# Value sums of the cross attention, head by head in four 32-column groups of TensorE

## The chip, the core and the metric

The kernel runs on one core of a Trainium2 chip. The engines are PE (TensorE: matmuls, with its weight loads shown apart as PEld), DVE (VectorE), ACT (ScalarE), POOL (GpSimd) and SP (SyncE, which only issues DMAs here). They run side by side and wait for each other through semaphores. The metric is the device time of one execution in microseconds (us).

## The reference, cut to what matters

A perceiver block on x [32, 32, 512] with a context of 257 rows per batch item: cross attention, then a causal linear attention, then a mixture of experts. Only the first part is touched:

```python
qm, km, vm = (_split_heads(...) for q, k, v)        # 16 heads of 32
scores = einsum('bnlh,bnph->bnlp', qm, km) / sqrt(32)
attn = softmax(scores, axis=-1)                     # over 257 context rows
out = einsum('bnlp,bnph->bnlh', attn, vm)           # <- the value sums
out = out.transpose(0, 2, 1, 3).reshape(B, L, 512)
return out @ Wo.T + bo
```

For each batch item and head, the value sums are a product of a [32 queries, 257] matrix of probabilities with [257, 32] values. Everything is fp32.

## The kernel before, in words

There are two stages. Stage A (to about 830 us) does both attentions, the router and part of the shared expert; stage B does the experts. Only stage A is touched.

Stage A walks over 32 batch items, as passes t of four items b, and each item has six steps k. Each engine has the same steps written out in order (`per_batch(t, b, k, ...)`), and behind a step stand pieces of later work (`on_post`, `on_pre`) at fixed places: the table POST says for instance that "oproj", the output projection of the four items of the pass before, comes at step 6, which is b=1, k=0. So the order on each engine is written by hand and does not adapt; the engines meet at semaphores alone.

For item n, steps 0 to 3 project the keys (lines 856 to 858: three matmuls of 256 moving columns with split weights), steps 4 and 5 the values (872 to 874). Softmax and value sums of an item are carried into the steps of the next. For the item before, DVE scales the probabilities (L599), PE transposes them (L840) in two halves j of 128 context rows, and ACT copies them out as `att[:, j, :]` (L473). `att` is [128 context rows, 2, 512], where the 512 columns are 16 heads x 32 queries. The values stand in `vb[pb]` as [128 context rows, 2, 512], where 512 is 16 heads x 32.

At k=5 PE forms the value sums. It takes four heads at a time, g = 0 to 3: 128 columns of values as weights and 128 columns of probabilities as the moving operand, first half j=0 (L888), then j=1 (L889) added to it. The product is 128 x 128: each of the four heads' values against each of the four heads' probabilities. Only the four 32 x 32 blocks on the diagonal are wanted. The last context row (257th) is held apart as a vector `vlc`, since the values are taken relative to that row. Right behind, PE computes two score matmuls of the current item (L901), for which DVE waits (L644).

DVE then reads the diagonal blocks in `attended`: four adds (L613), each on 32 partitions and 4 x 32 elements, of the block and `vlc`, into `ot`, the operand of oproj (L946). PE waits for `s_od` (`av_copied`) before oproj and before the value sums of the next item overwrite the accumulator `av_ps`. One wait of PE for DVE's adds stands also in the shared expert's L1013, which uses the same bank at the end of stage A.

Of the kernel before, what the change touches and what calls it, by code (L numbers as in the profile page):

```python
# [21 lines left out]
ALU = mybir.AluOpType  # L22
# [3 lines left out]
P = 128  # L26
NB, L, D = 32, 32, 512
S = 257
S1 = S - 1
DC = D // P  # L30
NH, HD = 16, 32
HG = P // HD
# [51 lines left out]
def wait(eng, sem, value, inc=None):  # L84


    if type(value) is int:
        if value > 0:
            eng.wait_ge(sem, value)
    else:  # L90
        eng.wait_ge(sem, value)
        if inc is not None:
            eng.sem_inc(inc, 1)


def stage_a(nc, d):


    with ExitStack() as ctx:
        def sb(name, shape, dt=F32):  # L100
            return ctx.enter_context(nc.sbuf_tensor(name, shape, dt))

        def sem(name):
            return ctx.enter_context(nc.semaphore(name))

        bank = [ctx.enter_context(nc.psum_tensor(f"bank{i}", [P, 512], F32)) for i in range(8)]
        kv_ps, sc_ps, at_ps, av_ps, px = bank[0:2], bank[2:4], bank[4], bank[5], bank[6:8]
# [23 lines left out]
        vb = [d.vb, sb("vb1", [P, 2, D])]  # L131
        nl = [sb(f"nl{i}", [P, DC]) for i in range(2)]
        vlc = sb("vlc", [P, DC, NB])
# [3 lines left out]
        att = sb("att", [P, 2, D])  # L137
        ot = sb("ot", [P, DC, P])
# [49 lines left out]
        s_tr, s_at, s_av, s_od = sem("probT_done"), sem("probT_copied"), sem("av_done"), sem("av_copied")  # L188
# [12 lines left out]
        tick = sem("tick")  # L201
# [320 lines left out]
        def _(dve):  # L522
            V = nc.vector
# [78 lines left out]
            def attended(t, b):  # L602

                n = BT * t + b - 1
                pb = (b - 1) % 4
                wait(dve, s_av, n + 1)
                if pb == 0:

                    t0 = t - 1 if b == 0 else t
                    wait(dve, s_px[BANK["oproj"]], (t0 - 1) * PER[BANK["oproj"]] + NTH["oproj"] + 1)  # L610
                for i in range(HG):
                    r = slice(i * HD, (i + 1) * HD)
                    ins = V.tensor_tensor(ot[r, :, pb * L:(pb + 1) * L],  # L613
                                          av_ps[r, :].rearrange("p (c n) -> p c n", c=DC)[:, :, i * HD:(i + 1) * HD],
                                          vlc[r, :, bass.ds(n, 1)].to_broadcast([HD, DC, L]), ALU.add)
                ins.then_inc(s_od, 1)

            def per_batch(t, b, k, front, nxt, prev):
                n = BT * t + b
# [16 lines left out]
                if k == 5 and carried:  # L636
                    attended(t, b)
# [139 lines left out]
            cnt, more, more2, end, start, own, picked, q4, col = d.cnt, d.more, d.more2, d.end, d.start, d.own, d.picked, d.q4, d.col  # L777
# [32 lines left out]
        def _(pe):  # L810
            mm, tr = nc.tensor.matmul, nc.tensor.transpose
# [31 lines left out]
            def per_batch(t, b, k, front, nxt, prev):  # L843
                n = BT * t + b
                carried = (front or b == 0) and (b > 0 or prev)
                h, lo = ch[b % 2], cl[b % 2]
# [3 lines left out]
                if k < 4 and front:  # L850
# [3 lines left out]
                    for c in range(DC):  # L854
                        w = slice(k * P, (k + 1) * P)
                        mm(out, wkh[:, c, w], h[:, c, :], start=c == 0, stop=False)  # L856
                        mm(out, wkh[:, c, w], lo[:, c, :], start=False, stop=False)  # L857
                        last = mm(out, wkl[:, c, w], h[:, c, :], start=False, stop=c == DC - 1)  # L858
# [7 lines left out]
                if k >= 4 and front:  # L866

                    wait(pe, s_ke, 4 * n + k - 1)
                    r = slice((k - 4) * P, (k - 3) * P)
                    out = kv_ps[k % 2][:, :]  # L870
                    for c in range(DC):
                        mm(out, h[:, c, r], wvh[:, c, :], start=c == 0, stop=False)  # L872
                        mm(out, h[:, c, r], wvl[:, c, :], start=False, stop=False)  # L873
                        last = mm(out, lo[:, c, r], wvh[:, c, :], start=False, stop=c == DC - 1)  # L874
# [6 lines left out]
                if k == 5 and carried:  # L881
                    wait(pe, s_at, 2 * n)
                    wait(pe, s_ve, 2 * n)
                    wait(pe, s_od, n - 1)
                    pb = (b - 1) % 2
                    for g in range(DC):
                        w = slice(g * P, (g + 1) * P)
                        mm(av_ps[:, w], vb[pb][:, 0, w], att[:, 0, w], start=True, stop=False)  # L888
                        last = mm(av_ps[:, w], vb[pb][:, 1, w], att[:, 1, w], start=False, stop=True)  # L889
                    last.then_inc(s_av, 1)  # L890
                if k >= 4 and front:
                    if k == 4:
# [88 lines left out]
            def on_shared(n, j):  # L981
# [24 lines left out]
                if n == "down":  # L1006
# [7 lines left out]
                    last.then_inc(s_sd, 1)  # L1014

            passes(pe, per_batch, on_post, on_pre, on_shared)

            pe.wait_ge(s_idx, NT)
# [665 lines left out]
```

## Time and profile before

| what | value |
|---|---|
| median of 3 runs | 1418.9 us (1415.56 to 1419.02) |
| the profiled execution: time / span | 1421.52 us / 1419.4 us |
| mean granted clock of TensorE | 0.981 |
| PE busy | 1324.6 us (93%) |
| PEld / DVE / ACT / POOL busy | 1020.0 / 774.0 / 632.2 / 392.0 us |

The page gives the busy time of each engine, then the same in 40 slices of 35.5 us. Its digit is the busy share in tenths; "PEclk" is the clock granted to TensorE in tenths of full speed, where 0.5 is its level of 1.2 GHz and 1.0 that of 2.4 GHz. In the rows, `bank` is any of the accumulator banks, `xN` a count of records, and "[1.28 <-DVE ot L613]" an idle time and what ended it. An fp32 matmul leaves two records on PE (and two weight loads on PEld). Matmuls are pipelined: a record's duration includes latency, and the distance from start to start is what one takes of PE's time.

### The profile page before, as it was taken

What the parts mean: (1) busy time and instruction counts of PE and PEld (TensorE: products, weight loads), DVE (VectorE), ACT (ScalarE), POOL (GpSimd) and SP (SyncE); (2) the same over time, 40 slices, a digit from 0 to 9 for tenths busy, and PEclk for the clock granted to TensorE, in tenths of its full rate; (3) what the DMA queues carried; (4) which work ended last, traced back from release to release, by engine and by line L of the source; (5) the groups of instructions that cost most, each with busy time, mean ns of one, the idle gap of its engine ahead of it and who ended that gap; (6) DMA issues with size and microseconds to landing.
All of it is one profiled execution on the core that took longest, in us unless ns stands there. A gap on an engine that the chain in (4) does not pass through costs nothing. (4 is left out here: it accounts for less than half of the span.)

```text
span 1419.4 us, 27453 instructions
## 1 busy us (share of the span) xinstructions
PE 1324.6 (93%) x7110; PEld 1020.0 (72%) x7111; DVE 774.0 (55%) x1808; ACT 632.2 (45%) x1320; POOL 392.0 (28%) x314
## 2 busy tenths in 40 slices
PE   5999999999999999999997888999999999999991
PEld 4888878888888878788886544676677676677670
DVE  4445565565655655655655354665655566655540
ACT  3443344353343433443532114466666566656650
POOL 0001020030030210200300303455555555756441
PEclk9999999999999999999999988999999999999996
DMA  5721110201111101101002105799999999999985
GB/s 199 281 98 32 31 48 17 62 16 39 38 32 31 46 16 31 47 16 54 24 1 71 56 23 208 220 324 324 339 297 303 267 339 306 358 289 314 265 219 87
DMA packets 67184, 204.71 MB, mean 144 GB/s; under 512 B 16047, under 2 KB 18351, under 8 KB 56768
## 3 DMA queue, kind: packets, MB, share of 16 engines
q1 hardware_dynamic: 43248, 159.71, 31.3%
q0 software_dynamic: 23888, 44.40, 14.9%
q8 instruction: 25, 0.41, 0.1%
q14 instruction: 23, 0.19, 0.0%
HBM read 177.26 MB, written 37.03 MB: 151 GB/s over the span
## 5 line engine op out<-in xcount | busy, mean ns | idle before, releaser
L370 POOL TENSOR_TENSOR rstd<-vep,half 128x1 f32<-128x1 f32 x32 | 17.8, 555 | 600.4 <-DVE vep L537 600.3
L856 PE MATMUL bank<-ch,wkh 128*128 128x256 f32 x512 | 160.6, 314 | 8.1 <-DVE cl L548 8.0
L458 ACT ACTIVATE kt<-bank,colb 128x256 f32<-128x256 f32 x128 | 60.5, 472 | 239.1 <-PE bank L858 238.8
L1494 PE MATMUL ebank<-guh,xth 128*128 128x512 f32 x380 | 154.7, 407 | 1.6 <-DVE xtl L1387 1.0
L1382 DVE TENSOR_TENSOR gul<-wgu,guh 128x2048 fp32r<-128x2048 f32 x54 | 123.8, 2293 | 55.3 <-ACT guh L1299 48.4
L1496 PE MATMUL ebank<-guh,xtl 128*128 128x512 f32 x380 | 149.0, 392 | 0.0
L1495 PE MATMUL ebank<-gul,xth 128*128 128x512 f32 x380 | 148.3, 390 | 0.0
L1229 POOL DMA_INDIRECT xg<-xn_rows,ig x95 | 121.3, 1277 | 85.1 <-issue 71.2
L858 PE MATMUL bank<-ch,wkl 128*128 128x256 f32 x512 | 144.3, 282 | 0.0
L857 PE MATMUL bank<-cl,wkh 128*128 128x256 f32 x512 | 144.2, 282 | 0.0
L1524 PE MATMUL ebank<-wd,ht 128*128 128x512 f32 x292 | 134.4, 593 | 0.8 <-ACT ht L1284 0.8
L856 PEld LDWEIGHTS bank<-ch,wkh 128*128 128x128 f32 x512 | 97.4, 190 | 16.1 <-issue 15.1
L1299 ACT CAST guh<-wgu 128x2048 fp32r<-128x2048 f32 x54 | 102.9, 1906 | 11.5 <-DMA wgu<-in_egu 11.5
L872 PE MATMUL bank<-wvh,ch 128*128 128x512 f32 x256 | 107.2, 419 | 0.0
L857 PEld LDWEIGHTS bank<-cl,wkh 128*128 128x128 f32 x512 | 97.5, 191 | 7.0 <-issue 6.7
L408 POOL DMA_INDIRECT slot_table<-entry,idx x61 | 60.3, 989 | 152.5 <-DVE idx L754 136.3
L874 PE MATMUL bank<-wvh,cl 128*128 128x512 f32 x256 | 101.5, 396 | 0.0
L873 PE MATMUL bank<-wvl,ch 128*128 128x512 f32 x256 | 100.9, 394 | 0.0
L1289 ACT ACTIVATE sg<-ebank 128x256 f32<-128x256 f32 x95 | 36.4, 384 | 139.4 <-PE ebank L1496 124.9
L858 PEld LDWEIGHTS bank<-ch,wkl 128*128 128x128 f32 x512 | 97.2, 190 | 0.0
L1377 DVE TENSOR_TENSOR h<-ebank,sg 128x256 f32<-128x256 f32 x95 | 40.0, 424 | 85.3 <-ACT sg L1289 72.9
L1524 PEld LDWEIGHTS ebank<-wd,ht 128*128 128x128 f32 x292 | 51.4, 190 | 45.2 <-issue 44.0
(247 smaller groups left out, 2817.2 us busy)
## 6 DMA issues: line engine op xcount, KB each, us to landing
wgu<-in_egu SPq DMA_DIRECT2D x54, 1024.0 KB
wd<-in_edn SPq DMA_DIRECT2D x54, 512.0 KB
sgu<-in_egu SPq DMA_DIRECT2D x17, 1024.0 KB
craw<-in_ctx SPq DMA_DIRECT2D x32, 514.0 KB, 3.2
sdn<-in_edn SPq DMA_DIRECT2D x17, 512.0 KB
wqkv<-in_wqkv SPq DMA_DIRECT2D x1, 3072.0 KB, 18.4
second_sums<-x1b SPq DMA_DIRECT2D x9, 256.0 KB, 3.7
xa<-in_x SPq DMA_DIRECT2D x8, 256.0 KB, 2.7
```

Of the source, the lines that this page charges most:

```text
L856: mm(out, wkh[:, c, w], h[:, c, :], start=c == 0, stop=False)
L857: mm(out, wkh[:, c, w], lo[:, c, :], start=False, stop=False)
L858: last = mm(out, wkl[:, c, w], h[:, c, :], start=False, stop=c == DC - 1)
L872: mm(out, h[:, c, r], wvh[:, c, :], start=c == 0, stop=False)
L874: last = mm(out, lo[:, c, r], wvh[:, c, :], start=False, stop=c == DC - 1)
L1229: nc.gpsimd.indirect_dma_start(tile.xg[item.q][:, :], None, d.xn, bass.IndirectOffsetOnAxis(ig[item.q][:, tile.half:tile.half + 1], 0), bo ...
L1299: nc.scalar.copy(guh[par][:, :, :], wgu[w][:, :, :]).then_inc(s_w["gu_high"], 1)
L1382: V.tensor_tensor(gul[par][:, :, :], wgu[w][:, :, :], guh[par][:, :, :].bitcast(F32), ALU.subtract).then_inc(s_w["gu_low"], 1)
L1494: mm(out, ah[:, c, :], bh[:, c, :], start=c == 0, stop=False)
L1495: mm(out, ah[:, c, :], bl[:, c, :], start=False, stop=False)
L1496: return mm(out, al[:, c, :], bh[:, c, :], start=False, stop=c == n - 1)
L1524: last = mm(y_ps[tile.half][:, :], tile.ht[:, c, :], wd[item.w][:, c, :], start=c == 0, stop=c == IC - 1)
```

## The change

PE: in place of 8 matmuls of 128 weight columns by 128 moving columns there are 32 of 32 by 32, one for each head and half of the context. Head i of a group of four writes to partitions 32i to 32i+31 and the columns of its group g, so that the result is dense: `av_ps[:, 0:128]`. Head after head of a group goes to another of the four column groups of the array. A semaphore increment stands ahead of the block. DVE: one add over all 128 partitions replaces the four. Semaphores, their values and all else stay.

```diff
@@ attended (DVE)
-                for i in range(HG):
-                    r = slice(i * HD, (i + 1) * HD)
-                    ins = V.tensor_tensor(ot[r, :, pb * L:(pb + 1) * L],
-                                          av_ps[r, :].rearrange("p (c n) -> p c n", c=DC)[:, :, i * HD:(i + 1) * HD],
-                                          vlc[r, :, bass.ds(n, 1)].to_broadcast([HD, DC, L]), ALU.add)
-                ins.then_inc(s_od, 1)
+                V.tensor_tensor(ot[:, :, pb * L:(pb + 1) * L], av_ps[:, 0:P].rearrange("p (c n) -> p c n", c=DC),
+                                vlc[:, :, bass.ds(n, 1)].to_broadcast([P, DC, L]), ALU.add).then_inc(s_od, 1)
@@ per_batch (PE), k == 5
+                    pe.sem_inc(tick, 1)
                     for g in range(DC):
-                        w = slice(g * P, (g + 1) * P)
-                        mm(av_ps[:, w], vb[pb][:, 0, w], att[:, 0, w], start=True, stop=False)
-                        last = mm(av_ps[:, w], vb[pb][:, 1, w], att[:, 1, w], start=False, stop=True)
+                        for j in range(2):
+                            for i in range(HG):
+                                h, at = g * HG + i, g * P + i * L
+                                last = mm(av_ps[i * HD:(i + 1) * HD, g * L:(g + 1) * L], vb[pb][:, j, h * HD:(h + 1) * HD], att[:, j, at:at + L],
+                                          start=j == 0, stop=j == 1)
                     last.then_inc(s_av, 1)
```

In PE's queue, around one block of the value sums in a pass t, before (`bank<-att,vb` are the value sums, `bank<-kt,qb` the scores, `bank<-ch,wkh` the keys of the next item):

```order
L874 MATMUL bank<-wvh,cl 128x512
L888 MATMUL bank<-att,vb 128x128
L889 MATMUL bank<-att,vb 128x128
L888 MATMUL bank<-att,vb 128x128
L889 MATMUL bank<-att,vb 128x128
L888 MATMUL bank<-att,vb 128x128
L889 MATMUL bank<-att,vb 128x128
L888 MATMUL bank<-att,vb 128x128
L889 MATMUL bank<-att,vb 128x128
L901 MATMUL bank<-kt,qb 128x257 x2
L856 MATMUL bank<-ch,wkh 128x256
```

and now, at the same place (line numbers are those of the changed kernel):

```order
L870 MATMUL bank<-wvh,cl 128x512
L887 MATMUL bank<-att,vb 32x32 x32
L900 MATMUL bank<-kt,qb 128x257 x2
L852 MATMUL bank<-ch,wkh 128x256
```

Nothing changed its place; the 8 instructions became 32. On DVE, behind the second input of the linear attention (`am`), before:

```order
L677 TENSOR_SCALAR am<-am 128x512
L613 TENSOR_TENSOR ot<-bank,vlc 32x4x32 x4
L644 TENSOR_TENSOR prob<-bank,cap 128x257 x2
```

and now:

```order
L673 TENSOR_SCALAR am<-am 128x512
L611 TENSOR_TENSOR ot<-bank,vlc 128x4x32
L640 TENSOR_TENSOR prob<-bank,cap 128x257 x2
```

Here too only the four adds became one, ahead of the same minima over the scores.

## Rows read from the trace of the kernel before

**Rows 1.** Page, parts 1 and 2: busy time, then tenths in 40 slices

```profile
PE 1324.6 (93%) x7110; PEld 1020.0 (72%) x7111; DVE 774.0 (55%) x1808; ACT 632.2 (45%) x1320; POOL 392.0 (28%) x314
...
PE   5999999999999999999997888999999999999991
...
PEclk9999999999999999999999988999999999999996
```

**Rows 2.** Busy time by stretch, 100 to 700 us; columns in its head

```profile
core 0: us, PE busy (x) PEld busy (x) DVE busy (x) ACT busy (x) POOL busy (x), PEclk, DMA share, GB/s
100.00:700.00 600.00, 585.79 (x3692) 491.86 (x3692) 348.54 (x892) 235.52 (x630) 80.82 (x87) 1.00 0.12 35
```

**Rows 3.** Waits of PE from 30 to 790 us, longest total first

```profile
engine line waited for: us in total, times, longest us
PE bank L946 <- DVE ot L613: 6.9, 6, 1.3
PE bank L975 <- ACT xt L495: 5.1, 7, 0.7
```

**Rows 4.** Timeline of PE behind the last batch, 788 to 800 us

```profile
start us, us, engine line op out<-in xcount [idle before <-releaser]
...
790.12 0.39 PE L889 MATMUL bank<-att,vb 128*128 128x128 f32 x2
794.42 2.91 PE L1013 MATMUL bank<-sdn,wq 128*128 128x512 f32 x4 [3.91 <-DVE ot L613]
```

**Rows 5.** Timeline of PE around one block of value sums

```profile
300.31 0.38 PE L888 MATMUL bank<-att,vb 128*128 128x128 f32 x2
...
302.09 1.03 PE L901 MATMUL bank<-kt,qb 128*128 128x257 f32 x4
302.77 0.47 PE L856 MATMUL bank<-ch,wkh 128*128 128x256 f32 x1
303.08 0.28 PE L857 MATMUL bank<-cl,wkh 128*128 128x256 f32 x1
303.20 0.28 PE L858 MATMUL bank<-ch,wkl 128*128 128x256 f32 x1
...
305.82 3.70 PE L946 MATMUL bank<-wo,ot 128*128 128x512 f32 x8 [1.28 <-DVE ot L613]
```

**Rows 6.** Line L888; duration is minimum, median, maximum in ns

```profile
engine op xcount: duration ns min/median/max, first and last start us, forms
L888 PE MATMUL bank<-att,vb x256: 270/275/377, 53.1 to 790.0; 128*128 128x128 f32 x128
```

**Rows 7.** Groups of DVE by form, the row of L613

```profile
L613 DVE TENSOR_TENSOR ot<-bank,vlc 32x128 f32<-32x128 f32 x128 | 36.7, 287 | 74.9 <-PE bank L889 62.6 <-remote 11.0
```

**Rows 8.** Timeline of PE from 35.5 us, and line L834

```profile
36.04 3.65 PE L834 MATMUL bank<-ctl,raw 128*128 128x32 f32 x32
...
L834 PE MATMUL bank<-ctl,raw x32: 191/276/276, 36.0 to 39.4; 128*128 128x32 f32 x32
```

**Rows 9.** Timeline of PE and line L1561, and the stretch around it

```profile
863.61 1.01 PE L1561 MATMUL ebank<-cn,col 128*1 128x64 f32 x8 [5.59 <-PEq L99]
...
L1561 PE MATMUL ebank<-cn,col x8: 263/311/311, 863.6 to 864.3; 128*1 128x64 f32 x8
...
863.00:866.00 3.00, 2.39 (x15) 2.20 (x16) 1.98 (x15) 0.30 (x1) 1.49 (x2) 0.50 0.43 101
```

**Rows 10.** Timeline of PE where it crosses from transposes to L872

```profile
297.43 0.47 PE L872 MATMUL bank<-wvh,ch 128*128 128x512 f32 x1
297.75 0.39 PE L873 MATMUL bank<-wvl,ch 128*128 128x512 f32 x1
297.98 0.39 PE L874 MATMUL bank<-wvh,cl 128*128 128x512 f32 x1
```

**Rows 11.** Timeline of DVE in the same batch

```profile
303.06 1.52 DVE L539 TENSOR_SCALAR xa<-xa,mv,rstd 128x512 f32<-128x512 f32 x1 [3.25 <-POOL rstd L370]
304.50 1.18 DVE L613 TENSOR_TENSOR ot<-bank,vlc 32x128 f32<-32x128 f32 x4
```

## The prediction

> **What bounds the kernel now.** I read the page's busy shares and slices first. PE is busy 93% of the span, and in slices 2 to 21 it stands at nine tenths or more at full granted clock [rows 1]. The change touches only the work before about 820 us, so I then took the busy times by stretch: from 100 to 700 us PE is busy 585.8 of 600 us, DVE 348.5, ACT 235.5, DMA 12% [rows 2]. In that stage every nanosecond added to or taken from PE's own stream counts in full, unless it fills one of the 14 us of gaps. The waits of PE name those gaps: the largest sum is 6.9 us in six waits, oproj (L946) waiting for the DVE adds of L613, the very adds that the change rewrites [rows 3]. One more such wait of 3.9 us stands behind the last batch, where L1013 waits for the same line [rows 4].
>
> **What the block costs today.** In the timeline of PE the block of value sums begins at 300.31 with its first L888 and the scores L901 begin at 302.09: 1.78 us [rows 5]. It is 8 matmuls; as fp32, each leaves two records (L888 runs 4 x 32 = 128 times and has 256), so 16 records at 111 ns start to start. The mean of one record, 275 ns, is a latency and not a price [rows 6]. There are 32 blocks (128 L613 records in fours [rows 7]): 57.0 us of PE's time.
>
> **What it costs after.** The change makes 32 matmuls of a block, each with 32 columns of weights and 32 moving columns, so 64 pairs of a weight load and a matmul where 16 stood. The arithmetic per pair falls to a quarter, the number of pairs rises fourfold: if pace followed columns alone, nothing would be won or lost. So all hangs on the pace of one small pair, and no row of before shows this form. The bounds from the nearest rows:
> - L834 has the same 32 moving columns but 128 columns of weights: 32 pairs in 3.65 us, the last 0.276 of it latency, so 3.37/31 = 109 ns [rows 8]. That is what the 128-column moving form takes too (111 ns), so L834 is held by its weight load, or by something that doesn't shrink at all. If all shrinks with the weight columns, 109 x 32/128 = 27 ns; if nothing does, 109 ns.
> - L1561 has one column of weights and 64 moving: 8 pairs in 1.01 us, of which 0.31 the latency of the last, so 0.70/7 = 100 ns, in a stretch of granted clock 0.50, the 1.2 GHz level [rows 9]. Were it held by the array's streaming alone, half the clock and twice the columns would make it 25 ns in the new form; halved for the clock alone it is 50 ns.
> I take 50 ns. It is the row nearest in shape (few weight columns, few moving ones) with the known factor of the clock taken off, and I don't take off the second factor, because a pair is two instructions that must each be issued, and nothing here shows issue at under 50 ns a pair. It also lies near the geometric middle of 27 and 109 (54). So 64 x 50 = 3.20 us for a block, 1.42 more than now; x 32 = **+45.4 us**. The ends: 64 x 27 = 1.73 us (-1.6 us in all) and 64 x 109 = 6.98 us (+166 us).
>
> The Trainium skill (TensorE: Matmul & The Clock Gate, section "Wait — 56ns, not 53.3ns?") says that starts of matmuls never come closer than about 25 ns however few columns they have. No run here shows it so far; for matmul and weight load together an estimate from that page is 50 ns if both pay that floor in turn, and 25 if the load hides: 3.20 or 1.60 us a block.
>
> **Entering and leaving the form, and the new instruction.** Ahead of the block stands a semaphore increment on PE that wasn't there; it now carries the waits for the copied probabilities, the values and the DVE adds. Queued behind it are the whole block and the scores L901, for which DVE waits. Where PE crosses a wait or another form now, the first pair costs more: L872 at 297.43 is followed at 297.75, 0.32 us, against 0.23 us in the run of such pairs: 0.09 us; L856 at 302.77 is followed at 303.08, 0.31 against 0.12: 0.19 us [rows 5, 10]. Bounds for both edges together 0 and 0.38 us; I take 0.2 x 32 = **+6.4 us**. The Trainium skill (TensorEngine Tiling (Array Packing), section "Tiling Modes") says that changing the tiling mode drains the engine; by it the edges would be nearer the upper bound, and the sum some 6 us more.
>
> **DVE.** Four adds on 32 partitions become one on 128. The four take 1.18 us [rows 11], one record 287 ns mean [rows 7], and the elements per partition stay 128, so the new one should take the same 0.29: 0.89 us less per batch, 28 us of DVE in all. DVE is not the bound, so this counts only in the waits of PE. In the case shown, DVE waited for rstd until 303.06, normed, began the adds at 304.50 and ended at 305.68; PE had been done with its 12 key matmuls and started oproj at 305.82, idle for 1.28 us [rows 5, 11]. After: adds done at 304.8, while PE comes to oproj 1.6 us later than before. The wait goes: **-6.9 us** for the six. The one at L1013 shrinks by the 0.9 us that the adds save [rows 4]: **-0.9 us**. Nothing else comes late in its place: ACT's copies and DVE's minima get 1.6 us more room per batch.
>
> Sum: +45.4 + 6.4 - 6.9 - 0.9 = +44.0. The profiled execution took 1421.5 us (span 1419.4), 2.6 above the median of 1418.9, so 1465.5 for it and **1463 us** in terms of the median.
>
> **Rivals.**
> - *The array's pace, 25 to 35 ns a pair, not side by side.* For it: L834 and the 128-column form have equal pace, as weight loads of equal width would give [rows 6, 8]. At 27 ns: -1.6 + 6.4 - 0.9, and the six oproj waits lose only the 0.88 of the adds each, -5.3: 1417.5. At 35 ns a block is 2.24 us: +14.7 + 6.4 - 7.8 = 1432. Against: it wants two instructions issued in 27 ns.
> - *Four at once: faster.* The four heads of a group go to four column groups, one after another in the stream. If their pairs overlap, a block takes 16 x 27 = 0.43 us, 1.35 less: -43.2 + 6.4. Then PE comes to oproj 1.35 earlier while DVE still starts its adds at 304.50, so each of those waits grows by 1.35 - 0.88 = 0.47, +2.8; with -0.9 it is -34.9, **1384 us**. It decides below about 25 ns a pair; the place is the stretch between the last L874 and the first L901. For it: a weight column group of its own for each head. Against: no two matmuls of before start under 100 ns apart. The Trainium skill's page on the clock gate, section "Part 3: Packing small matmuls — row/col tiling", states this rule, with starts about 4 ns apart between tiles; no run here shows it so far.
> - *A floor that hardly shrinks, over 75 ns a pair.* For it: three forms of very different arithmetic (32, 64 and 128 moving columns; 1 and 128 weight columns) all stand at 100 to 111 ns [rows 5, 8, 9]. At 80 ns: 5.12 us a block, +106.9 + 6.4 - 7.8 = 1524; at 109: +166.4 - 1.4 = 1584.
>
> **Chances.** 35 to 75 ns (the forecast's mechanism, issue of the pairs) 47%; 25 to 35 ns 23%; over 75 ns 16%; under 25 ns 14%. This measurement tells 0.3%, 4.3 us, from no change, so "same" is 1414.6 to 1423.2, which is a pace of about 26 to 30 ns: 11%. Faster: the four-at-once case and the edge of the next, 15%. Slower 74%. The range goes from 1405, where only the overlap case is left out, to 1545 (90 ns a pair: 5.76 us, +127.4 - 1.4 = 1545). The forecast's own range, 35 to 75 ns, is 1432 to 1514.
>
> **What would show it.** The stretch from the first matmul of the block to the next L901: 3.2 us says issue at 50 ns, 1.7 the array's pace, 0.4 to 0.8 overlap, over 5 the floor. The next matmul after L901 says the cost of the form's edge. The adds should be one DVE record of about 0.29 us, and the row of PE waiting for them at oproj should be gone; if it stays, PE isn't late. The granted clock should stay 1.00 from 100 to 700 us. I am wrong if the pace of a pair is not between 35 and 75 ns, or if PE idles elsewhere for what it gained or lost.

## The result

The changed kernel takes 1406.7 us (median of 5 runs, 1403.8 to 1409.8) against 1418.9 (5 runs) for the kernel before on the same chip: 0.9919 of its time, 95% interval 0.9898 to 0.9940. So it is 0.8% faster, 12 us, where 44 us slower was forecast. The profiled execution took 1406.7 us, its span is 1404.6 against 1419.4: 14.8 us to be explained. In two later groups of runs the same kernel was 0.9 and 1.2% slower than before; that is the last experiment below. Three executions of the third group below took 4772, 4770 and 2226 us; its ratios leave them out.

The page of the changed kernel, parts 1 to 3, answers to [rows 1]:

```profile
PE 1307.1 (93%) x8646; PEld 994.0 (71%) x8647; DVE 746.3 (53%) x1712; ACT 631.4 (45%) x1320; POOL 396.4 (28%) x314
...
PE   5999999899899899899998987999999999999991
...
PEclk9999999999999999999998988999999999999996
...
q8 instruction: 67, 1.10, 0.3%
```

PE has 1536 matmuls more and is busy 17.5 us less; its row of slices shows an 8 at even distances, four times, where [rows 1] has nines (the 8s at slices 8, 11, 14 and 17). The row of q8, packets that bring instructions, is to be kept in mind: it read `q8 instruction: 25, 0.41, 0.1%` in the kernel before.

PE's timeline around one block of value sums, and DVE's add for it, answer to [rows 5, 11] (start us, duration us, engine, line):

```profile
295.37 0.40 PE L870 MATMUL bank<-wvh,cl 128*128 128x512 f32 x1
295.70 0.76 PE L887 MATMUL bank<-att,vb 128*32 128x32 f32 x64
296.39 1.14 PE L900 MATMUL bank<-kt,qb 128*128 128x257 f32 x4
297.18 0.47 PE L852 MATMUL bank<-ch,wkh 128*128 128x256 f32 x1
...
298.77 3.60 PE L945 MATMUL bank<-wo,ot 128*128 128x512 f32 x8
```

```profile
295.81 1.50 DVE L539 TENSOR_SCALAR xa<-xa,mv,rstd 128x512 f32<-128x512 f32 x1 [0.79 <-POOL rstd L370]
297.24 0.28 DVE L611 TENSOR_TENSOR ot<-bank,vlc 128x128 f32<-128x128 f32 x1
```

The 64 small pairs take 0.69 us from the first to the scores, not 3.20. A pair's record lasts 196 ns at the median, so 63 distances fit into 0.76 - 0.196 = 0.564 us: **9.0 ns a pair**. The matmul before the block in the kernel before was this one:

```profile
300.08 0.39 PE L874 MATMUL bank<-wvh,cl 128*128 128x512 f32 x1
```

The rows of the waits from 30 to 790 us (us in total, times, longest) and the work behind the last batch answer to [rows 3, 4]:

```profile
PE bank L852 <- issue: 13.8, 4, 3.6
PE bank L974 <- ACT xt L495: 5.0, 7, 0.7
...
PE bank L1012 <- DVE ot L611: 0.7, 1, 0.7
PE bank L945 <- DVE ot L611: 0.4, 1, 0.4
```

```profile
781.20 1.96 PE L1012 MATMUL bank<-sdn,wq 128*128 128x512 f32 x4 [0.70 <-DVE ot L611]
```

Both waits for the adds are nearly gone: 6.9 to 0.4 us and 3.9 to 0.7. In their place stands a row that had no counterpart: four idle times of up to 3.6 us at L852, put down to "issue", that is, to nothing that the profile shows. One of them in PE's timeline:

```profile
275.90 0.39 PE L977 MATMUL bank<-msum,cn 128*128 128x64 f32 x2
279.56 0.58 PE L852 MATMUL bank<-ch,wkh 128*128 128x256 f32 x1 [3.28 <-issue]
279.94 0.42 PE L853 MATMUL bank<-cl,wkh 128*128 128x256 f32 x1
...
287.80 0.40 PE L868 MATMUL bank<-wvh,ch 128*128 128x512 f32 x1
```

L977 is the last matmul of one round of PE's loop over t, L852 the first of the next. The clock around it, against [rows 2] (columns as there):

```profile
100.00:700.00 600.00, 578.11 (x4932) 477.14 (x4933) 329.60 (x825) 238.17 (x640) 81.81 (x89) 0.98 0.12 36
279.56:285.06 5.50, 5.50 (x26) 5.50 (x26) 0.89 (x3) 1.45 (x5) 3.02 (x4) 0.50 0.04 6
286.00:291.50 5.50, 5.50 (x36) 4.84 (x35) 1.61 (x6) 4.46 (x14) 3.83 (x4) 1.00 0.02 1
```

PE stood idle for 3.28 us, and its first 5.5 us of work behind that ran at granted clock 0.50, the 1.2 GHz level. The granted clock over 100 to 700 us is 0.98 where it was 1.00.

The sum, by places, from these rows and [rows 3 to 5]:

| place | before | after | in all, us |
|---|---|---|---|
| last value-projection matmul to first small pair | 0.23 | 0.33 | +3.2 |
| block of value sums, start to scores | 1.78 | 0.69 | -34.9 |
| scores to keys (L852) | 0.68 | 0.79 | +3.5 |
| oproj waits for DVE | 6.9 | 0.4 | -6.5 |
| wait behind the last batch | 3.9 | 0.7 | -3.2 |
| four jumps back, idle and slow clock | 0 | 4 x 5.9 | +23.7 |

(The first three are times 32, as if each block were the one shown; in the trace nearly all are within 0.01 us of it.) Together -14.2 of the 14.8 seen. The 5.9 of a jump is worked out with the first experiment.

### The profile page after: what moved, and what is told of

Its sections match the earlier page's. It is cut to its first block and busy times, and to the rows that moved or that the text cites. A ratio compares the mean times of both kernels' runs of the same rounds, so it can differ in the third digit from the quotient of the medians.

```text
span 1404.6 us, 30400 instructions
## 1 busy us (share of the span) xinstructions
PE 1307.1 (93%) x8646; PEld 994.0 (71%) x8647; DVE 746.3 (53%) x1712; ACT 631.4 (45%) x1320; POOL 396.4 (28%) x314
## 5 line engine op out<-in xcount | busy, mean ns | idle before, releaser
L852 PE MATMUL bank<-ch,wkh 128*128 128x256 f32 x512 | 165.5, 323 | 22.0 <-issue 13.8
L458 ACT ACTIVATE kt<-bank,colb 128x256 f32<-128x256 f32 x128 | 60.7, 474 | 261.8 <-PE bank L854 261.7
L1228 POOL DMA_INDIRECT xg<-xn_rows,ig x95 | 126.6, 1333 | 85.5 <-issue 71.8
L854 PE MATMUL bank<-ch,wkl 128*128 128x256 f32 x512 | 149.1, 291 | 0.0
L853 PE MATMUL bank<-cl,wkh 128*128 128x256 f32 x512 | 149.1, 291 | 0.0
L852 PEld LDWEIGHTS bank<-ch,wkh 128*128 128x128 f32 x512 | 102.8, 201 | 29.9 <-issue 29.6
L868 PE MATMUL bank<-wvh,ch 128*128 128x512 f32 x256 | 107.9, 422 | 0.0
L853 PEld LDWEIGHTS bank<-cl,wkh 128*128 128x128 f32 x512 | 102.9, 201 | 7.0 <-issue 6.7
L854 PEld LDWEIGHTS bank<-ch,wkl 128*128 128x128 f32 x512 | 102.2, 200 | 0.0
L548 DVE SCALAR_TENSOR_TENSOR cl<-craw,nl,ch 128x256 fp32r<-128x256 f32 x128 | 53.4, 479 | 57.3 <-ACT ch L425 57.3
## 6 DMA issues: line engine op xcount, KB each, us to landing
wqkv<-in_wqkv SPq DMA_DIRECT2D x1, 3072.0 KB, 18.6
```

Of the source, the lines that this page charges most:

```text
L1228: nc.gpsimd.indirect_dma_start(tile.xg[item.q][:, :], None, d.xn, bass.IndirectOffsetOnAxis(ig[item.q][:, tile.half:tile.half + 1], 0), bo ...
```

## The experiments

Each kernel was timed beside the kernel before on the same chip. The runs form six groups; ratios are to the kernel before of the same group, whose median was 1417.9 in the first, 1421.1, 1421.9 and 1421.1 in the second to fourth, 1416.5 and 1417.3 in the last two. Line numbers of the variants differ by a few.

### Is it the jump back? (first group)

Theory: the loop's body has become too long to be kept, so that each jump back waits for instructions. Rival: something else at the seam of the rounds, where one round of the loop ends and the next begins, idles PE. *after_unrolled* writes the five rounds of PE's loop out; *before_unrolled* does the same to the kernel before, as a control:

```diff
-            with eng.Fori(2, NT - 1) as t:
-                body(True, True, t, True, per_batch, on_post, on_pre)
+            for t in range(2, NT - 1):      # PE alone
+                body(True, True, t, True, per_batch, on_post, on_pre)
```

> The changed kernel with PE's own loop over passes 2 to 6 written out; all other engines keep their loop, and PE's instructions and their order stay the same. Theory (the jump back costs): PE's loop body has grown past what the core holds of PE's instructions, so each of the four jumps back waits 3.3 to 3.6 us for instructions, and 5.5 us of matmuls behind it run at the 1.2 GHz level, where they take 2.5 us more: 5.9 us each, 24 us in all. Written out, the four idle times in front of L852 with nothing that released them are gone, the granted clock is 1.00 from 100 to 700 us, and the time is 1406.7 - 24 = 1383. Rival (the idle times belong to something at that place in the pass, such as the pos step or a semaphore): they stay, and the time is 1407.

> The kernel before with the same loop of PE written out: the control. Theory: before, no jump back stood idle and no instruction block was fetched in the loop, so nothing is won: 1419, within 0.3%. Rival (written-out passes are faster anyway, because waits against registers become waits against constants): 1419 less what the first run gains, some 1395 to 1410, and then the gain of the first run says nothing about fetching.

Measured: 1382.4 us, ratio 0.9738 (0.9722 to 0.9754), and 1416.3, 0.9983 (0.9967 to 0.9999). The same seam in the written-out changed kernel (timeline of PE), and its stretch of 100 to 700 us:

```profile
275.39 0.39 PE L981 MATMUL bank<-msum,cn 128*128 128x64 f32 x2
275.58 0.36 PE L856 MATMUL bank<-ch,wkh 128*128 128x256 f32 x1
...
281.37 0.40 PE L872 MATMUL bank<-wvh,ch 128*128 128x512 f32 x1
```

```profile
100.00:700.00 600.00, 590.49 (x5133) 485.24 (x5132) 341.81 (x852) 245.12 (x658) 81.88 (x89) 1.00 0.13 36
```

From the last matmul of a round to the first of the next it is 0.19 us instead of 3.66, so the idle time costs 3.47; and the 48 key matmuls behind it take 5.79 us instead of 8.24, so the clock costs 2.45. That is 5.9 a jump, 23.7 us for four: 1406.7 - 23.7 = 1383, and 1382.4 was measured. The granted clock is 1.00 throughout. Writing the loop out does little for the kernel before, which has no such idle times. What is left of the wait for DVE at oproj, and DVE and PE at the same block as above, which begins here at 289.27:

```profile
PE bank L949 <- DVE ot L615: 1.7, 5, 0.4
```

```profile
291.09 1.51 DVE L543 TENSOR_SCALAR xa<-xa,mv,rstd 128x512 f32<-128x512 f32 x1 [2.50 <-POOL rstd L374]
```

```profile
292.86 3.70 PE L949 MATMUL bank<-wo,ot 128*128 128x512 f32 x8 [0.33 <-DVE ot L615]
```

So without the jumps the wait comes back in part. DVE's norm begins 1.82 us behind the block's start, not 0.11: it waits for `rstd` from POOL, which had just issued its eight indirect transfers. The 5.9 us that PE loses at a jump give POOL and DVE that much time to be ready.

### How much body is too much?

*half_new* uses the new form in every second batch only (the other batches keep the old 8 matmuls and the four adds), with the loop kept; *before_repeated* keeps the old form but runs each block four times, which adds as many instructions to the body as the change does:

```diff
+                    if b % 2:
+                        for g in range(DC):     # the old two matmuls for each g
+                            ...
+                    for g in range(0 if b % 2 else DC):   # the new form
```

```diff
-                    for g in range(DC):
+                    for g in [g for _ in range(4) for g in range(DC)]:
```

> Two of the four blocks in a pass (items b = 0 and 2) in the new form with one add of DVE, two (b = 1 and 3) in the old form with four adds. PE's loop body then stands halfway between the two kernels. Theory (size of the body): if halfway still fits, no idle time at the jump back and no fetches in the loop; the gain is half of what the form gives without the stalls (1419 - 1383 = 36, so 18): 1401. Rival (the stall comes with the 32-column form or with the semaphore increment): four idle times of some 3.4 us stay, and the time is 1419 - 18 + 24 = 1425.

> The kernel before, still with its loop, with the 8 matmuls of each block of value sums issued four times over (the same result again): 32 matmuls in the old 128-column form, so PE's loop body is as long as that of the changed kernel, less the semaphore increment. Theory (length of the body): four idle times before the first key matmul L856 with no releaser appear at the jumps back, of 3 to 4 us, with instruction blocks fetched in the loop (67 packets in all, as in the changed kernel), and the clock falls behind each; time 1419 + 32 x 24 x 0.223 = 1590, and 24 more: 1614. Rival (the stall needs the 32-column form or the increment): none of these, 25 packets, 1590.

Measured: *half_new* 1399.5, ratio 0.9875 (0.9852 to 0.9898), with no idle time at the seam. *before_repeated*, a single run in the second group, 1605.3 beside 1421.1 (1614 was expected), with this row among PE's waits, and one of the four in its timeline:

```profile
PE bank L856 <- issue: 5.5, 4, 1.6
```

```profile
470.65 0.38 PE L856 MATMUL bank<-ch,wkh 128*128 128x256 f32 x1 [1.58 <-issue]
```

So the old form stalls at the same four jumps once its body is that long, 1.2 to 1.6 us at a time where the new form has 3.3 to 3.6. Its first matmul behind a jump takes 0.38 or 0.39 us, not 0.58; the granted clock over some 5 us behind each of the four is 1.00, so it didn't fall there. That is not all that it loses. Some 10 us behind two of its jumps PE stands idle again, up to 3.2 us (`PE bank L840 <- issue: 4.8, 3, 3.2`, where the kernel before has 1.2), and it waits longer for ACT's `att`. Whether these belong to the fetches or to the interruptions of the last experiment, which fall into the same part of a round, was not separated. The packets of q8, in the order *before_unrolled*, *after_unrolled*, *half_new*, *before_repeated*:

```profile
q8 instruction: 44, 0.72, 0.2%
```

```profile
q8 instruction: 56, 0.92, 0.3%
```

```profile
q8 instruction: 28, 0.46, 0.1%
```

```profile
q8 instruction: 67, 1.10, 0.3%
```

These rows can be counted through. The two written-out kernels differ by 3072 instructions of the new form (1536 matmuls, 1536 loads) and by 12 packets: 256 instructions each. Four more bodies of the kernel before cost 44 - 25 = 19 packets, so its body has about 1216 instructions; the change adds 4 x 96 = 384: 1600; the half form 1408. Fetched once, the changed kernel would need 25 + 4.5 + 1.5 = 31 packets (12 batches outside the loop, 4 in it); it has 67, so 36 too many: 9 at each of four jumps back. A body of about 1408 instructions is kept and nothing is fetched; one of about 1600 is not. The DMA rows say the same by time: from 290 to 670 us q8 brings 32 packets in the changed kernel and none in the kernel before or in *half_new*. In the changed kernel one packet comes at 275.0 to 275.5 us, still ahead of the jump, the next between 276.3 and 277.0, when PE is already idle, and another between 279.5 and 279.7, where PE starts again. The written-out form brings 27 packets from 290 to 670 us and has no such idle time: fetching ahead of need costs nothing that can be seen, fetching that starts at the jump does.

The Trainium skill (Runtime: NRT & Kernel Launch, section "Instruction fetch mechanics") says that PE holds 2048 instructions, refilled in blocks of 256, and that a taken branch whose target lies outside the two blocks at hand forces a fetch. The packet size agrees with the rows. The two limits don't: by two blocks the kernel before, at about 1216, would fetch at each jump, and it fetches nothing; by 2048 the changed kernel would be kept, and about 1600 are already too many. That the fetch runs ahead of the execution and pushes out the start of the body would fit the packet ahead of the jump and 9 packets for a body of 6.25, but was not shown.

### The pace: how many column groups at once?

*same_group* has the very instructions of the change, in an order in which each column group's 16 pairs stand in a row; *two_groups* alternates between two groups, in the written-out form; *head_pairs* takes two heads at once, 64 columns wide in two groups, 32 pairs to a block (half of its output is not the wanted product; the loop is kept, with four adds). *same_group* ran in the first group, *two_groups* in the second, *head_pairs* in the fourth:

```diff
-                    for g in range(DC):
-                        for j in range(2):
-                            for i in range(HG):
+                    for i in range(HG):
+                        for g in range(DC):
+                            for j in range(2):
```

```diff
+                    for i2, g in [(i2, g) for i2 in range(2) for g in range(DC)]:
+                        for j in range(2):
+                            for i in (2 * i2, 2 * i2 + 1):
```

```diff
+                            for i in range(2):
+                                w = slice(g * P + i * 64, g * P + (i + 1) * 64)
+                                last = mm(av_ps[i * 64:(i + 1) * 64, g * 64:(g + 1) * 64], vb[pb][:, j, w], att[:, j, w], ...)
```

> The changed kernel with the 32 matmuls of a block in another order: all eight of one head position i first, so that eight in a row go to the same column group, and only then the next group. Same matmuls, same count. Theory (side by side): a pair takes 11 ns only because neighbours go to different column groups; in one group a pair must take its 32 weight columns and its 64 moving cycles, at least 27 ns, so a block takes 1.7 us instead of 0.69, and the kernel 32 us more: 1439. Rival (a small pair takes 11 ns wherever it goes): the block stays at 0.7 us and the time at 1407.

> The same base, with the matmuls ordered so that they alternate between two column groups (0 and 1, then 2 and 3) where they went round all four. If a group is held for 27 ns by its pair and groups are otherwise free, two groups give 13.5 ns a pair, 0.2 us more a block than the 10 to 11 ns of four: 1388. If 27/4 = 6.7 ns were the law for four, the 9 to 11 ns measured would be another floor (issue), which 13.5 lies above, so the same 1388. Rival (any change of group is enough): 1382.

> The changed kernel (PE's loop kept) with two heads to a matmul: 16 matmuls of 64 weight columns by 64 moving columns in a block, alternating between two groups of 64 columns, and four adds of DVE on the diagonal blocks. Twice the arithmetic of the heads one by one, half the instructions: the loop body grows by 8 matmuls a block and not by 24. Theory: 53 ns for 64 weight columns, two groups side by side, so 27 ns a pair and 0.9 us a block (before 1.78, changed 0.69), edges as in the changed kernel: 0.73 us less than before a block, 23 in all, and no idle time at the jumps back, no blocks fetched in the loop: 1419 - 23 = 1396. Rival (what counts is heads one by one, pairs don't overlap): 32 pairs at 53 ns, 1.7 us a block, 1419.

PE's timeline in the three, one block each:

```profile
304.96 1.91 PE L887 MATMUL bank<-att,vb 128*32 128x32 f32 x64
306.80 0.70 PE L900 MATMUL bank<-kt,qb 128*128 128x257 f32 x2
```

(with `PE bank L852 <- issue: 9.5, 4, 2.6` among its waits)

```profile
281.12 1.11 PE L891 MATMUL bank<-att,vb 128*32 128x32 f32 x64
```

```profile
278.39 1.15 PE L891 MATMUL bank<-att,vb 128*64 128x64 f32 x32
```

Worked out as above, a pair comes every 27 ns in one group ((1.91 - 0.196)/63), every 14.5 in two and every 9.0 in four. 27 ns is just the 109 x 32/128 of the prediction's lower bound [rows 8]: nothing holds a pair at 50. It is also near the 25 that L1561 gives if its moving columns and its clock are both taken off [rows 9]. Weight and moving columns are equal in number in all three kernels, so they don't tell which of the two sets the 27. Two groups bring nearly the half of it, four the third, not the quarter (6.8). A 64-wide pair in two groups comes every (1.15 - 0.222)/31, about 30 ns (0.222 us is its record), where 109/2/2 would be 27. In all: *same_group* 1429.9, ratio 1.0074 (1.0057 to 1.0091), slower than before with the same instructions. It stayed under the 1439 expected: its blocks cost 36.8 us more than those of the changed kernel, but its idle times at the jumps are 4.3 less, and its granted clock from 100 to 700 us is 0.99, not 0.98, by an estimate worth up to 6 us. That leads to 1433; the four executions took 1428.6 to 1434.3. *two_groups* came to 1417.4, 0.9967 (0.9952 to 0.9982), and *head_pairs* to 1417.5, 0.9977 (0.9955 to 0.9998), where 1388 and 1396 were expected. These two ran where blocks were interrupted, as the last experiment tells (*head_pairs* has `PE bank L891 <- issue: 7.6, 15, 0.9`), and their totals can't be set against the first group. Against *no_increment*, which goes round four groups and ran beside it, *two_groups* is 13.8 us slower; the blocks account for 11.2 (32 x 0.35). The gain is in the order round the four groups.

### The increment and the one add

*no_increment* takes the new `pe.sem_inc` out of the written-out form; *four_adds* puts the four adds on 32 partitions back, on the new layout:

```diff
-                    pe.sem_inc(tick, 1)
```

```diff
-                V.tensor_tensor(ot[:, :, pb * L:(pb + 1) * L], av_ps[:, 0:P]...)
+                for i in range(HG):
+                    r = slice(i * HD, (i + 1) * HD)
+                    ins = V.tensor_tensor(ot[r, :, pb * L:(pb + 1) * L], av_ps[r, 0:P]...)
```

> The changed kernel with PE's loop written out (the base of this and the next two, 1382.4 us), without the semaphore increment ahead of each block; the waits then sit on the first matmul. Rival 1 (the increment is the edge): the first small matmul follows the last value matmul by 0.23 us and not 0.32, 32 x 0.09 = 3 us less: 1379. Rival 2 (the edge is the change of form): it stays at 0.32 us, and 1382.

> The same base, with DVE's one add on 128 partitions split into four on 32 partitions each, reading the same dense result: the DVE part of the change undone alone. Theory: each costs about 0.28 us more, 0.88 a batch, which shows only where PE stands at oproj; its wait of 0.33 us there becomes 1.2, seven or eight times: 6 to 7 us more, 1389. Rival (DVE's adds are hidden): 1382.

Measured: 1403.6 (0.9871, 0.9837 to 0.9905) and 1416.4 (0.9967, 0.9951 to 0.9983). Neither can be set against the 1382.4 of the first group, as the next part shows. Within PE's timeline *no_increment* answers its own question, since the edge into the new form is still 0.33 us:

```profile
276.44 0.40 PE L874 MATMUL bank<-wvh,cl 128*128 128x512 f32 x1
276.77 0.76 PE L890 MATMUL bank<-att,vb 128*32 128x32 f32 x64
```

The 0.10 us over the usual 0.23 belongs to the change of form, and the increment costs nothing that can be seen. For the adds see the end of the next part.

### The same kernel, 20 to 30 us apart

All three small-pair kernels of the second group came out 20 to 30 us above what the first had led to expect. So the written-out form, the one with four adds, the changed kernel itself, the half form and the kernel before were each run again, unaltered:

> The changed kernel with PE's loop written out, once more, beside the next one on one chip. In the three variants of it (no increment, four adds, two groups) the block of the item b = 0 took 3.3 to 3.9 us instead of 0.6 in nearly every pass, with idle time inside the block that nothing released; in this kernel, measured on another chip, it didn't. Theory A (the chip or its state decides): if the next kernel is slow in these blocks, this one is too, some 1400 to 1415 us. Theory B (the kernel decides, by when the block meets the context load and the instruction fetch): this one stays at 1382 with all 32 blocks at 0.6 us while the next is at 1416.

> The four adds on the written-out base, once more. Theory A: where the kernel above has no idle time inside its blocks, this has none either, and comes out at 1382 to 1389. Theory B: 1416 again, with blocks of 3.6 to 3.9 us in each pass at b = 0.

> The changed kernel as it is, on the same chip. Theory A and B both: four idle times of 3.3 to 3.6 us at the jumps back, 1407; if the chip makes blocks slow, these come on top: up to 1440.

> Half the blocks in the new form, once more, beside the changed kernel. Its loop body fits and fetches nothing in the loop. If the 20 to 30 us that some groups of runs add to the changed kernel come from instructions fetched late while POOL's indirect transfers run, this kernel stays at 0.985 to 0.99 of the kernel before wherever it runs (1399 where before is 1418). If they come from anything else, it loses as well: 1405 to 1420.

> The changed kernel, a third time, to see how it stands beside the two above: 0.992 of before as in the first measurement, or 1.012 as in the second. In the second case I expect idle times without releaser in b = 0 of the passes, as there; in the first only the four at the jumps back.

> The kernel before, profiled beside the three above. By the theory of late instruction fetches it is the same everywhere within 0.3% in the passes of the loop, where it fetches nothing; what it loses (1418 against 1421 so far) is outside them, before 190 us and after 690 us.

| kernel | first result | later | ratio later |
|---|---|---|---|
| before | 1417.9 | 1421.9, 1421.9 | 1.0000 (0.9982 to 1.0017) |
| changed | 1406.7 | 1436.7, 1435.9 | 1.0121 (1.0087 to 1.0155), 1.0091 (1.0059 to 1.0122) |
| changed, written out | 1382.4 | 1402.7 | 0.9861 (0.9832 to 0.9890) |
| half new | 1399.5 | 1429.0 | 1.0046 (1.0027 to 1.0066) |
| written out, four adds | 1416.4 | 1415.7 | 0.9959 (0.9945 to 0.9973) |

The kernel before moved by 3 us or so, those with small pairs by 20 to 30; the form with four adds did not move, but its first result is itself of the second group. The groups fall into two kinds: in the second to fourth the kernel before stands at 1421.1 to 1421.9 and the others lose time, in the rest it stands at 1416.5 to 1418.9 and they don't. One chip gave both kinds of result. Where the time goes stands in PE's timeline; here is one block of *half_new* in its second run, which took 3.84 us where the undisturbed ones take 0.69:

```profile
298.96 0.66 PE L901 MATMUL bank<-att,vb 128*32 128x32 f32 x22
300.85 0.20 PE L901 MATMUL bank<-att,vb 128*32 128x32 f32 x1 [1.23 <-issue]
302.26 0.61 PE L901 MATMUL bank<-att,vb 128*32 128x32 f32 x41 [1.21 <-issue]
302.80 1.66 PE L914 MATMUL bank<-kt,qb 128*128 128x257 f32 x4
```

The burst of small pairs is interrupted twice, for 1.2 us each, with no semaphore to wait for. In this run the blocks of b = 0 are hit, one in each round from 190 us on, and no others until the last. The idle times are not the whole loss. *half_new* has 13.6 us of them and a span 30.3 us longer than in its first run; the granted clock from 100 to 700 us, 1.00 then, is now 0.98, which by an estimate from these two rows is worth up to 12 us more:

```profile
100.00:700.00 600.00, 578.36 (x4281) 480.85 (x4280) 335.21 (x846) 231.27 (x621) 81.08 (x87) 0.98 0.12 35
```

The rows of waits of the same kernel, of *unrolled_again* and of *changed_again* (30 to 790 us):

```profile
PE bank L901 <- issue: 13.6, 18, 1.2
```

```profile
PE bank L891 <- issue: 16.9, 23, 1.3
```

```profile
PE bank L836 <- ACT att L473: 18.6, 8, 5.2
PE bank L852 <- issue: 13.5, 4, 3.6
...
PE bank L887 <- issue: 3.6, 5, 1.2
```

It isn't the jump back: the half form fetches nothing in its loop (28 packets in both runs) and the written-out form has none. In the changed kernel most of it shows at L836, where PE waits for ACT, 18.6 us in all against 3.1 in the first run: ACT is late as well. In the round shown above PE's first L868 comes at 288.01 us where it was at 287.80, but ACT's copy of the last keys ahead of it (L458) at 291.97 where it was at 288.00. So more than PE's small pairs is held up. I suspected the transfers that POOL starts in that part of a round, and moved its scatter of a round some 10 us later, into the next round's "oproj", in the written-out form:

```diff
-                if n == "pos":
+                if n == "pos" and type(t) is int and t == NT - 1:
                     scatter(t)
...
+                    scatter(t - 1)      # in "oproj", behind x1b, for all t > 0
```

> The changed kernel with PE's loop written out, and POOL's eight indirect transfers of a pass (slot_table, the pos step) moved: POOL issues them some 10 us later, behind x1b in the next pass, so that they no longer run beside the block of value sums of b = 0. The idle times inside a block have come only in that block, where these transfers and the context load run. Theory (POOL's transfers hold up the burst of small pairs): no block with idle time inside, 1382 even where the kernel below is at 1403. Rival (the context load, or the place in the pass): the idle times stay at b = 0, 1400.

> The changed kernel with PE's loop written out, on the same chip as the run above, as its base: 1382 with 32 blocks of 0.6 us, or 1403 with the seven or eight blocks of b = 0 at 3.4 us. Only in the second case does the run above tell anything.

> The kernel with POOL's transfers moved, once more, on another chip. If the kernel before stands at 1421 here, as it did wherever the small matmuls lost time, then theory (POOL's transfers hold up the burst): 0.974 of before, about 1384, no idle time inside a block; rival: 0.986, about 1402, idle times at b = 0. If before stands at 1417, both give 1382 and the run tells nothing on this.

Measured: 1381.4 (0.9741, 0.9709 to 0.9774), 1384.1 for the written-out form unmoved (0.9760, 0.9726 to 0.9793), and 1379.6 (0.9741, 0.9717 to 0.9766). None of the three had the interruptions, the unmoved one neither, so the disturbance wasn't there to be removed, and whether these transfers cause it stays open; the context load, which runs at the same time, was not tested at all. The 2.7 us between the first two is less than their intervals.

For the adds two groups hold a pair of kernels, both with the interruptions: in the third 1415.7 with four against 1402.7 with one, in the second 1416.4 against the 1403.6 of *no_increment*. So with the interruptions the four adds cost 13 us, twice the 6 to 7 expected; what they cost without them was not measured. In *four_adds_again* PE also waits 1.8 us for the copied keys, which the other has no row for, and its interrupted blocks take 3.97 to 4.08 us where those of *unrolled_again* take 3.45 to 3.74, some 3 us in all; the rest of the 13 us is not accounted for.

The written-out form of the change beats both kernels in every group where it ran: 0.974 to 0.976 undisturbed, 0.986 disturbed. Apart from its variant with the moved transfers, which can't be told from it by these runs, it is the best version found.

## Why the prediction was wrong

The step that failed is the pace of a small pair. "I take 50 ns", it says, because "a pair is two instructions that must each be issued, and nothing here shows issue at under 50 ns a pair". That no row shows a thing at under 50 ns doesn't bound it: every row of before was held by 128 weight columns or by half the clock, so none of them could show the issue of instructions. L1561 with the clock taken off [rows 9] was no measurement of issue either, and its second factor should have been taken off too. The runs put 27 ns in one column group, the lower bound of the prediction, and 9.0 with four groups: neighbouring pairs in different column groups overlap, which the forecast's sum left out. The term of +45.4 us was -34.9.

Point by point:
- **PE bounds the stage, every ns counts**: right. The sum by places on PE's own stream gives the change of the span within 0.6 us.
- **Today's block, 1.78 us**: right, the kernel with the old form and its control bear it out.
- **Edges, +6.4**: right in size, +3.2 and +3.5, 0.21 us a block. The cause was given too broadly: the increment has no part in it. By the Trainium skill's rule on draining (TensorEngine Tiling (Array Packing), section "Tiling Modes") it would have been nearer 0.38; the rows say 0.21.
- **The wait at oproj, -6.9**: -6.5, but for another reason, so the size was luck. The prediction had it vanish because PE would come later. PE comes 0.9 us earlier, and DVE is earlier still. For this case the rival "four at once" had the wait grow by 2.8 us, taking DVE's start as fixed. It isn't: DVE begins its norm (L539) 0.11 us behind the block's start where it was 2.75 before [rows 5, 11], and its add is over at 297.5, PE at oproj at 298.77. In part the jump back does it, where POOL and DVE gain on PE: in the written-out form the norm begins 1.82 us behind the start and 1.7 us of the wait are left.
- **L1013, -0.9**: -3.2. I had counted the adds' 0.9 us alone; where the other 2.3 us come from is open.
- **The granted clock stays at 1.00**: wrong, 0.98, by the four jumps; written out it is 1.00.
- **The rivals.** "Four at once" had the mechanism, in the place that it named. That its 1384 us is nearly what the written-out form takes (1382.4) is in part luck: it had the blocks at -43.2 where they were -34.9, and the wait at oproj at +2.8 where it was -5.2. It had a chance of 14% because "no two matmuls of before start under 100 ns apart", the same argument as above. The Trainium skill (TensorE: Matmul & The Clock Gate, section "Part 3: Packing small matmuls — row/col tiling") had stated it; its 4 ns between starts isn't reached with weight loads in between, 9.0 is. The same page's floor of about 25 ns (section "Wait — 56ns, not 53.3ns?") is contradicted by the block's row, so for neighbours in different column groups it doesn't hold. "The array's pace, not side by side" is what *same_group* runs: 27 ns and 1429.9, 12.4 above its 1417.5, of which 9.5 are the idle times at the same four jumps; behind three of these the clock also fell.
- **What no rival had**: the length of the loop's body. I priced the 48 more pairs of each batch in time and never as instructions that have to be held. It gives back 23.7 of the 38 us that everything else gained.

The time fell just inside the range's lower end (1405) in the first comparison, and it did so by luck, as a sum of two effects that the range wasn't made from.

## What to carry to other kernels

- Small fp32 matmuls should be ordered so that neighbours use different column groups: the same instructions cost 27 ns a pair in one group and 9 in four. Price one pair by its columns (here weight and moving columns were equal in number), then divide by less than the number of groups (27 ns became 14.5 in two and 9.0 in four), and don't read a floor from rows that something else holds.
- Whoever multiplies the instructions of a looped body counts them: when packets on the instruction queue rise by a fixed number with each round, the jumps back may show as idle times with no releaser, and the clock behind them may be the lower one, as it was here behind 3.3 us. Writing the loop out took both away here, and so did a shorter body.
- The kernels with small pairs varied more between groups of runs than the one they replace; one comparison, however tight its interval, tells of its own group.

## What the runs showed of the hardware

- Pairs of weight load and matmul, fp32, 32 by 32, 128 rows: 27 ns in one column group, 14.5 in two, 9.0 in four. The step into the form takes 0.10 us more (0.33 against 0.23), and the scores behind it 0.11 more (0.79 against 0.68).
- The body of PE's loop was kept at about 1408 instructions and not at about 1600. With each jump back 9 packets of 256 instructions were then fetched again, and PE stood idle at the jump for 3.3 to 3.6 us in the new form, 2.1 to 2.6 in *same_group* and 1.2 to 1.6 in the old form with as many instructions. Fewer idle microseconds go with slower pairs; why is open.
- After 3.28 us of idling PE's granted clock stood at 0.50 for its first 5.5 us of work, and key matmuls that take 5.79 us took 8.24; after the 1.2 to 1.6 us at the jumps of *before_repeated* it stayed at 1.00.
- Idle times of up to 1.3 us inside bursts of small pairs, 13.6 to 16.9 us in a run of *half_new* and of the written-out form, with 20 to 30 us lost in all, in three of the six groups of runs and not in the others, on one and the same chip either way. Their cause is open.
